# Layer 1: the second half of the short key tile's scores is issued one turn sooner on TensorE

## The reference, cut to what matters

```python
q, k = rmsnorm(x @ Wq.T), rmsnorm(context @ Wk.T)     # 32 heads of 8
v = context @ Wv.T
p = softmax(q @ k.T / sqrt(8))                        # 256 x 1601 for a head
x = x + gate * (p @ v)
x = x + gate * ffn(layernorm(x))
```

## Time and profile before

| | us |
|---|---|
| three runs, median (lowest to highest) | 1708.33 (1707.88 to 1710.69) |
| the profiled execution, its own time | 1710.15 |
| span of its profile | 1708.3 |
| PE busy (share of the span) | 1614.5 (95%) |
| ACT busy | 1377.0 (81%) |
| DVE busy | 1396.7 (82%) |
| POOL busy | 1148.3 (67%) |

### The profile page before, as it was taken

The page is one execution under the profiler, slowest core; times in us unless marked ns, Lnnn a source line. Parts: engine busy times, 40 slices in busy tenths (PEclk is TensorE's granted clock), DMA queues, the critical chain, the costliest instruction groups (busy, mean ns, idle before and its releaser), DMA issues. The chain is left out here.

```text
span 1708.3 us, 44057 instructions
## 1 busy us (share of the span) xinstructions
PE 1614.5 (95%) x16022; PEld 1013.2 (59%) x16022; DVE 1396.7 (82%) x3493; ACT 1377.0 (81%) x2311; POOL 1148.3 (67%) x1770
## 2 busy tenths in 40 slices
PE   3799999999999999999999999998898999999997
PEld 2466777677777677767777777766554333333332
DVE  8889999899999999999988888888996755655422
ACT  4688888788887788888887888884336999999996
POOL 3558778787787877888787778875765655646200
PEclk8799999999999999999999999998999999999998
DMA  4299999999899998999999999997423222222100
GB/s 176 79 183 198 201 209 196 184 223 207 209 192 194 199 194 187 212 218 201 207 187 210 223 207 193 217 190 167 141 44 115 45 51 72 45 38 45 33 8 14
DMA packets 608872, 261.11 MB, mean 153 GB/s; under 512 B 576528, under 2 KB 581648, under 8 KB 607248
## 3 DMA queue, kind: packets, MB, share of 16 engines
q1 hardware_dynamic: 604432, 258.05, 70.7%
q10 hardware_dynamic: 4224, 0.25, 0.2%
HBM read 99.15 MB, written 17.29 MB: 68 GB/s over the span
## 5 line engine op out<-in xcount | busy, mean ns | idle before, releaser
L1754 PE MATMUL pv<-PT,VV 128*128 128x256 bf16 (+1 forms) x2880 | 342.7, 276 | 11.5 <-DMA PT<-PB 11.4
L1734 PE MATMUL score<-KK,QT 128*128 128x512 bf16 (+2 forms) x1920 | 341.9, 323 | 5.6 <-DVE mxp L1229 5.2
L1494 ACT ACTIVATE PB<-S,rsum 128x1024 bf16<-128x1024 f32 (+1 forms) x256 | 246.5, 988 | 105.2 <-DVE rsum L1260 82.4
L1754 PEld LDWEIGHTS pv<-PT,VV 128*128 128x128 bf16 (+1 forms) x2880 | 282.1, 99 | 80.1 <-issue 32.0
L1251 DVE SCALAR_TENSOR_TENSOR PB<-S,rsum,PB 128x1024 bf16<-128x1024 f32 (+1 forms) x256 | 296.4, 1159 | 3.2 <-ACT PB L1494 3.2
L1734 PEld LDWEIGHTS score<-KK,QT 128*128 128x128 bf16 x1920 | 158.3, 98 | 143.3 <-DVE mxp L1229 11.2
L1484 ACT ACTIVATE S<-S,nmx 128x1601 f32<-128x1601 f32 x128 | 210.1, 1642 | 8.6 <-DVE nmx L1241 8.5
L2634 ACT ACTIVATE P<-score 128x1024 f32<-128x1024 f32 x196 | 197.8, 1053 | 5.0 <-PE score L2726 3.5
L1072 POOL TENSOR_SCALAR S<-S,rsum 128x256 f32<-128x256 f32 x128 | 73.9, 578 | 125.5 <-DVE rsum L1260 113.2
L1613 PE MATMUL tb<-stage,wsb 128*128 128x512 bf16 (+1 forms) x768 | 150.0, 339 | 5.2 <-DVE stage L631 3.9
L2746 PE MATMUL pv<-P,V 128*9 128x256 f32 (+1 forms) x2288 | 153.5, 383 | 0.3 <-ACT P L2634 0.3
(11 more groups left out here) (274 smaller groups left out, 3690.0 us busy)
## 6 DMA issues: line engine op xcount, KB each, us to landing
x<-rs_d SPq DMA_DIRECT2D x16, 936.0 KB, 5.1
rsb<-rs_d SPq DMA_DIRECT2D x16, 936.0 KB, 5.4
wsb<-w_split SPq DMA_DIRECT2D x46, 256.0 KB, 4.7
wsb<-w_split SPq DMA_DIRECT2D x23, 512.0 KB, 5.0
wpr<-in_wprojT SPq DMA_DIRECT2D x23, 512.0 KB, 6.6
context_d<-stage SPq DMA_DIRECT2D x16, 400.2 KB, 4.1
l_ctx<-context_d SPq DMA_DIRECT2D x4, 1601.0 KB, 7.3
rawh<-in_w_all SPq DMA_DIRECT2D x12, 512.0 KB, 5.5
```

What stands on the lines that cost most here:

```text
L1494: e.activation(m.PB[n % 2][:, 2 * a:a + b], m.S32[n % 2][:, a:b], ACT.Copy, scale=m.rsum[n % 2][:, 1:2]).then_inc(s["p_hi"], 1)
L1734: i = e.matmul(m.score[:, at:at + b - a], qt[:, kind, qp, q * P:(q + 1) * P], kk[:, kp, a:b], start=(k == 0), stop=(k == 2))
L1754: i = e.matmul(m.pv[:, at:at + 256], vv[0:rows, v, t, :], m.PT[k % 2][0:rows, turned(c, a), :], start=(c == first and r == 0), stop=(c == ...
```

## The change

The scores of half 1 of the short turn (u = 6) are no longer issued first in turn 6 but in turn 5, behind `times_v` and ahead of what is prepared there. Nothing else changes, on no other engine.

```diff
         b, u, h = n // L1T, n % L1T, n // L1U - 1
-        if n < B * L1T:
+        if n < B * L1T and u % L1U < L1U - 1:
             scores(b, u, 1)
         if n + 1 < B * L1T:
             scores((n + 1) // L1T, (n + 1) % L1T, 0)
         if n:
             times_v((n - 1) // L1T, (n - 1) % L1T, 0)
             times_v((n - 1) // L1T, (n - 1) % L1T, 1)
+        if n + 1 < B * L1T and u % L1U == L1U - 2:
+            scores(b, u + 1, 1)
         for what, made, c in prepared(n):
             pe_prepare(e, m, s, made, what, c)
```

## The result

| | before | after |
|---|---|---|
| median of 22 runs each (us) | 1708.36 | 1714.38 |
| lowest to highest | 1702.9 to 1714.59 | 1706.45 to 1720.91 |
| span of the profiled execution | 1708.3 | 1710.8 |
| layer 1, from the start of its first exponential to 0.50 behind the start of its last | 395.0 | 400.1 |

The change makes the kernel slower: the ratio is 1.0033, with a 95% interval of 1.0023 to 1.0044, or 5.6 us (3.9 to 7.5). The lowest end of that interval, 0.23%, is still above the 0.2% that the prediction took as its bound for no change. Single runs of the two kernels overlap widely, so it takes the 22 of each to tell. The middle of the interval lies over the forecast of +4.5 by about one; the median itself is 1714.38 where 1712.8 was forecast.

A forecast was written before the change was run, and what follows sets the result against it. It took PE to bound the middle groups and ACT the last batch; 3.57 + 0.33 + 0.63 = 4.5 us slower, from the median 1708.33 to 1712.8 us. Its own range was 1711.3 to 1714.5, the full range 1709.4 to 1716.6.

The forecast's parts named there:

- first chain of waits: Middle of layer 1: PE from end to end, with no share of ACT or of waiting.
- second chain: Last batch, where nothing is prepared: ACT and issue, no PE.
- The price of a place: Each spot where the two short scores stand alone between pv and pa: 0.21 us on PE, bounds 0.10 and 0.34.
- The company: Short scores ran beside the next group's four, which need two rounds anyway; separated, they add one round and one change.
- Groups 1 to 6 of the second and third batch: PE-bound, pa behind: 0.21 us each; with groups 2 to 6 of the first batch, 17 x 0.21 = 3.57.
- Group 1's place: First batch: the delay runs into pv, which waits 0.45 us for DVE; 0.21 hidden, cost 0.
- Groups 1, 3 and 5 of the last batch: Next group's second full exponential starts 0.21 us later and ACT keeps the delay: 3 x 0.21 = 0.63.
- Groups 0 of the first three batches: PE's own small wait between the scores takes up 0.10 us: 3 x (0.21 - 0.10) = 0.33.
- The sum: All 24 places together: 3.57 + 0.33 + 0.63 = 4.5 us slower.
- rival 3: Every place: a block of scores costs a fixed 0.33 us whatever it holds; 7.3 us slower, 1715.6; chance 0.14.
- 1 (ACT is the bound): ACT's removed waits come back as time, at most 5.1 us faster: 1703.2; chance 0.09.
- 2 (the round slips in, 0.10): Short round slips under pv's end or pa's start, 0.10 us per place; 2.0 us slower, 1710.3; chance 0.19.

The follow-up runs named there:

- base_act_longer: The base with half 0's short exponential over 1024 columns instead of 512 in the first three batches; layer 1 395.3 us, 0.4 more than the base.
- base_last_only: The base with the short scores moved in the last batch only; a pair of its groups takes 24.98 us where the base has 24.76.
- four_in_one: The base with a different edit in each of the four batches of queries, read by group lengths in one run.
- batch 3: In four_in_one: the change's order on the base, half 1's short matmuls issued twice where they stand alone; middle group 12.59 us.
- batch 1: In four_in_one: on the base, half 1's short scores issued between the two matmuls of pa; middle group 12.58 or 12.59 us.
- base_switch_only: The base with pa between the two halves of the products with values in turn 5, no matmul added; middle group 12.43 us, 0.17 more.
- batch 2: In four_in_one: the base's order, half 1's short matmuls issued twice beside the next group's scores; middle group 12.27 or 12.28 us.
- the base: The kernel before with its transposing DMAs replaced by plain ones of the same tiles, only times read; 1703.43 us against 1710.34 for the kernel before.
- base_change: The same change made on the base; 1707.99 us, layer 1 399.9 us, 5.0 more than the base.

## Why the prediction was right

**What bounds the kernel.** In a middle group it is PE: base_act_longer adds 10 us of work to ACT for 1.0 us at most. The first chain of waits in the earlier trace rows, which had no ACT in it, said so before. In the last batch ACT is the bound only of the groups without a product. The prediction read its second chain in the earlier trace rows for the whole batch, but that stretch holds group 2 alone; ahead of it, at the place of the change, the chain runs through PE. This did no harm, as the prediction took PE's order there too and gave the delay on to ACT. base_last_only shows it: the batch gets slower though ACT's largest wait is removed.

**The price of a place.** Forecast 0.21, with bounds of 0.10 and 0.34; measured 0.22 a group, 0.23 from step to step. Its two parts can now be told apart: a round by itself is 0.11 (batch 3 of four_in_one against the change, 12.59 - 12.48), and one more change of the kind of work 0.11 (what is left of 0.22), 0.10 (batch 1) or up to 0.17 (base_switch_only). The second part had only been argued from the step of 0.20 to 0.22 in the earlier trace rows; it is shown by the two kernels that add a change and no round. The Trainium skill, TensorEngine Tiling (Array Packing), Key Properties, says that a change of tiling mode drains TensorE. The traces agree so far as each further change cost 0.10 to 0.17 us here; that the time goes into a drain they don't show.

**The company.** That the short scores cost nothing before, because they run beside two rounds that are there anyway, is shown by batch 2 against batch 3 of four_in_one: the same two extra matmuls are free in company (0.01 at most) and cost 0.11 alone.

**The places.** From one second full exponential to the next (the table in the section on the result) they can be read one by one.

- Groups 1 to 6 of the second and third batch: +0.22 each, all twelve between 0.217 and 0.224. Forecast 0.21.
- The first batch: groups 3 to 6 are longer by 0.22, 0.22, 0.30 and 0.22. Group 5's 0.08 above the others comes back on the base (+0.32) and isn't explained. Group 1's place is hidden, as foreseen: counted from layer 1's first exponential, the exponentials of after are late by 0.09 at the end of group 1, by 0.31 at group 2's second, and by 0.09 again from group 2's sixth on, behind DVE's wait of the earlier trace rows. Group 2's own place then puts 0.22 on again, which is why group 2 takes 12.78 both before and after.
- Groups 1, 3 and 5 of the last batch: forecast 0.63, measured 0.66, in the place foreseen. That the next group's second full exponential is late was foreseen; that its first is late as well, by 0.31, was not.
- Groups 0 of the first three batches were costed at 0.11 each. The second batch's is the steady one, 0.13 in both pairs of runs. The first batch's +0.17 and the third's +0.34 are smaller than what the same group 0 moves by from run to run.

**The sum.** 5.04 us in layer 1 for a forecast of 4.5. Without the groups 0 it is 4.40 for a forecast of 4.20, and 4.43 on the base. So the mechanism was right, and the price of a place was undersized by 0.01. The other 0.3 us lies in the groups 0, most of it in the third batch's: in the trace of after half 0's short scores start 0.30 behind the scores ahead of them (1507.19, 1507.49) and the step to pv is 0.53, where before has 0.10 (1507.04, 1507.14) and 0.32. In base_change this did not come again (group 0 is 11.99 there, group 1 12.69, against 12.09 and 12.80), so it is not the change's, and what held those scores stays open. The 5.6 us of the timed runs hold 5.0 well inside their interval, and the 0.6 between is no more than that interval.

**What the total can't say.** The interval of 3.9 to 7.5 us holds the forecast of 4.5 and also the 7.3 of rival 3, and the median of 1714.38 is nearer to rival 3's 1715.6 than to 1712.8. That the total came out in the forecast's range decides nothing between the two. The groups do: rival 3 would make a middle group 12.59, and it is 12.48.

**The rivals.** 1 (ACT is the bound): rejected, above. 2 (the round slips in, 0.10): rejected, 0.22. 3 (a block has a fixed price of 0.33, whatever it holds): rejected, a block of two takes 0.23 and one of four by itself 0.34 (1553.86 to 1554.20 in four_in_one).

**What stays open.** The 0.05 us of base_switch_only over its forecast, the 0.08 of the first batch's group 5, and what held the scores of the third batch's group 0 in after. And the order that does better: spreading the last products took 2.4 us from the last batch on the base. On the kernel before itself it wasn't run. An estimate from the same pairs (in the last batch of the kernel before such a pair takes 12.94 or 12.95 and 11.82 too) is 2.4 of 1708 us, 0.14%, below what a measurement of this kernel can tell.

## What to carry to other kernels

A wait on an engine that isn't the bound was worth nothing here, though the profile lists it 20 times. First see whether it stands in the chain of waits, in the very stretch that changes, then ask what moving the releasing work costs the engine that does. A mark that the change itself moves shifts time between neighbours; read groups from a mark that both kernels reach in the same way. Small matmuls on separate row strips rode for free on TensorE beside others that need as many rounds (0.01 us at most); out of that company they cost their own round, 0.11, plus one more change of the kind of work, another 0.11. Where a wait did lie on the path, in the last batch, it paid on the base to move the long work ahead of it to another turn, and not the short work past it.

## What the runs showed of the hardware

- By their recorded starts, matmuls on different row strips need not start in the order of issue: in batch 2 of four_in_one the second pair of half 1's short scores, issued first, starts at 1443.04, behind the first pair of half 0 at 1442.92. Eight matmuls on four strips take 0.34, two rounds.
- A round of 256 columns is 0.11; one more change between strips of 32 rows, strips of 32 columns and full width adds 0.10 to 0.17, by the three orders that were run. A pa matmul against 512 columns lasts 0.32 from its start to the scores behind it, two of them 0.54: by the difference 0.22 is the matmul itself.
- ACT's full exponentials last 1.02 to 1.10 but start every 0.91 where nothing is late, and short ones 0.59 to 0.62 for a step of 0.48: the start steps, not the durations, say how much ACT can do in a group here.
